# Linear attention in a four-stage fp32 block: values and state as the stationary operand, denominators from running key sums

## The reference

```python
h = _ln(x, g1, beta1)
q = _phi((h @ wq).reshape(b, s, H, DH), proj)     # _phi(x, proj) = elu(x @ proj) + 1
k = _phi((h @ wk).reshape(b, s, H, DH), proj)     # H = 16 heads, DH = 64
v = (h @ wv).reshape(b, s, H, DH)
def step(carry, qkv_t):                           # over the 1024 positions
    kv, ksum = carry
    kv = kv + k_t[..., :, None] * v_t[..., None, :]
    ksum = ksum + k_t
    num = jnp.einsum('bhd,bhde->bhe', q_t, kv)
    den = jnp.einsum('bhd,bhd->bh', q_t, ksum) + 1e-06
    return ((kv, ksum), num / den[..., None])
x = x + outs.reshape(b, s, H * DH) @ wo
```

## Time and profile before

| | |
|---|---|
| median of 3 runs | 3996.98 us (3996.84 to 3997.35) |
| profiled execution, its own time | 3997.76 us |
| its span, first to last instruction | 3995.9 us |
| linear attention, first to last instruction of its loop | 1353 to 2177 us |
| one turn in the steady part | 25.83 us |
| TensorE busy, whole span | 3643.4 us (91%) |
| VectorE, ScalarE, GpSimd busy, whole span | 2522.0, 1601.5, 1392.0 us |

### The profile page before, as it was taken

The page is one execution under the profiler, slowest core; times in us unless marked ns, Lnnn a source line. Parts: engine busy times, 40 slices in busy tenths (PEclk is TensorE's granted clock), DMA queues, the critical chain, the costliest instruction groups (busy, mean ns, idle before and its releaser), DMA issues. The chain is left out here.

```text
span 3995.9 us, 59179 instructions
## 1 busy us (share of the span) xinstructions
PE 3643.4 (91%) x21704; PEld 2593.4 (65%) x21704; DVE 2522.0 (63%) x5386; ACT 1601.5 (40%) x3052; POOL 1392.0 (35%) x1567
## 2 busy tenths in 40 slices
PE   6888878887799999999998998999979989999799
PEld 3666666666455688888886664666645556666465
DVE  4898988899566455555554444777743357777333
ACT  5666666666100122222221213666631146666211
POOL 4778777788100000000000223444411134444111
PEclk8899999999899999999998998999989999999899
DMA  1000000000200100000001112111122011111221
GB/s 39 1 11 12 1 11 11 11 6 6 87 32 32 35 12 12 12 12 12 11 11 55 64 63 64 38 34 37 38 63 64 27 59 33 38 34 34 74 64 37
DMA packets 150197, 129.32 MB, mean 32 GB/s; under 512 B 20804, under 2 KB 147544, under 8 KB 149656
## 3 DMA queue, kind: packets, MB, share of 16 engines
q1 hardware_dynamic: 149912, 125.54, 10.0%
HBM read 87.73 MB, written 37.77 MB: 31 GB/s over the span
## 5 line engine op out<-in xcount | busy, mean ns | idle before, releaser
L830 PEld LDWEIGHTS ssm_pu<-ident,ssm_ub 128*128 128x128 f32 x2048 | 255.8, 150 | 220.3 <-issue 86.0
L830 PE MATMUL ssm_pu<-ident,ssm_ub 128*128 128x128 f32 x2048 | 325.4, 292 | 80.4 <-POOL ssm_ub L322 47.2
L322 POOL TENSOR_SCALAR ssm_ub<-ssm_uT,ssm_bcT 128x512 f32<-128x512 f32 x512 | 356.4, 718 | 96.7 <-ACT ssm_uT L380 63.4
L336 POOL TENSOR_TENSOR ssm_acc<-ssm_acc,ssm_weighted 128x512 f32<-128x512 f32 x256 | 328.4, 1292 | 143.4 <-ACT ssm_weighted L462 143.0
L842 PE MATMUL ssm_pt<-ident,ssm_state 128*128 128x128 f32 x2048 | 288.5, 285 | 82.6 <-DVE ssm_acc L630 58.6
L2256 PE MATMUL win_pa<-win_w_wqkv,win_hT 128*128 128x512 f32 x768 | 357.9, 603 | 1.6 <-ACT win_hT L2043 1.1
L620 DVE TENSOR_TENSOR_SCAN ssm_state<-ssm_da,ssm_carry,ssm_pu 128x512 f32<-128x512 f32 x256 | 312.2, 1260 | 21.2 <-PE ssm_pu L830 16.4
L1838 PE MATMUL glu_up<-glu_hT,glu_w_w 128*128 128x512 f32 x704 | 309.4, 599 | 3.4 <-DVE glu_hT L1761 3.4
L620 DVE TENSOR_TENSOR_SCAN ssm_state<-ssm_da,ssm_pu 128x512 f32<-128x512 f32 x256 | 296.6, 1199 | 25.1 <-PE ssm_pu L830 16.9
L842 PEld LDWEIGHTS ssm_pt<-ident,ssm_state 128*128 128x128 f32 x2048 | 240.4, 147 | 107.9 <-DVE ssm_acc L630 67.8
L2017 POOL TENSOR_TENSOR win_rotated<-win_straight,win_turned 128x512 f32<-128x512 f32 x128 | 163.0, 1274 | 417.0 <-DVE win_turned L2132 417.0
(11 more groups left out here) (241 smaller groups left out, 7295.3 us busy)
## 6 DMA issues: line engine op xcount, KB each, us to landing
win_raw<-in_tables SPq DMA_DIRECT2D x64, 128.0 KB, 2.2
a<-win_y SPq DMA_DIRECT2D x64, 128.0 KB, 1.7
glu_xs<-a SPq DMA_DIRECT2D x32, 256.0 KB, 3.3
glu_x<-a SPq DMA_DIRECT2D x16, 512.0 KB, 5.3
ssm_x<-in_L_attn_x SPq DMA_DIRECT2D x8, 512.0 KB, 3.9
x<-ssm_out SPq DMA_DIRECT2D x16, 256.0 KB, 2.1
moe_x<-x SPq DMA_DIRECT2D x8, 512.0 KB, 3.9
x<-moe_y SPq DMA_DIRECT2D x8, 512.0 KB, 2.9
```

The source lines that it names most:

```text
L322: nc.gpsimd.tensor_scalar(ub[:, i % 2, t, :], uT[:, k % 2, t, :], bcT[:, k % 2, t, n:n + 1], 1.0, ALU.mult, ALU.mult).then_inc(ub_ready.se ...
L336: nc.gpsimd.tensor_tensor(acc[:, k % 2, t, :], acc[:, k % 2, t, :], weighted[:, j, :], ALU.add)\
L830: last = nc.tensor.transpose(pu[c][:, t * P:(t + 1) * P], ub[:, i % 2, t, c * P:(c + 1) * P], ident)
```

## The change

The operands of the numerator products change places. `state[:, r, :]` (now 128x128, 8 blocks of a pair each, off-diagonal halves zero) and `v` (now 64 columns a head) are the stationary operand, queries and scores are the moving one, and the result has features on partitions already. So the turning of `attn` on TensorE and its copy on ScalarE go, and `attn` with them: VectorE writes `attnT` from PSUM with one multiply for each bank of four pairs.

The denominators get a path of their own. VectorE keeps running sums of the keys along the positions (`key_sums`, 8 scans of 128x128 a turn, carried over from the turn before). GpSimd multiplies them with the queries (`weigh_sums`, 2 instructions of 128x512). TensorE adds over the features of each head with a constant 0/1 matrix `of_head` as the stationary operand, 16 columns wide: 8 products, result 16x128. VectorE adds 1e-6 and takes the reciprocal of 16x128. SP sends that to DRAM (8 KB), waits, and loads it back so that each of a pair's 64 partitions has its head's row (two DMAs of 64x8x128, 256 KB each). The multiply waits for both.

`keep` and its loads go: the factor is a constant 0.0 or 1.0 of the instruction. State growth on VectorE is 2 instructions of 64x512 in place of 6 smaller ones. The new tiles lie in `wT`, which is free after the folding of the weights.

The core of the diff:

```diff
+            def widen_reciprocals(turn):
+                sp.wait_ge(rden_ready.sem, rden_ready.at(turn.i))
+                sp.dma_start(rden_sent, rden[:, :]).then_inc(rden_out, 16)
+                sp.wait_ge(rden_out, 16 * (turn.i + 1))
+                sp.wait_ge(attn_ready.sem, attn_ready.at(turn.i - 1))
+                for j in range(2):
+                    sp.dma_start(rden_rows[j * DH:(j + 1) * DH, :, :],
+                                 rden_sent[j:H1:2, :].partition_broadcast(DH)).then_inc(rden_in, 16)
...
+            def weigh_sums(turn):
+                if turn.i:
+                    pool.wait_ge(den_made.sem, den_made.at(turn.i - 1))
+                for g in range(2):
+                    pool.wait_ge(sums_made.sem, sums_made.at(turn.i, g + 1))
+                    pairs = slice(g * GP, (g + 1) * GP)
+                    nc.gpsimd.tensor_tensor(q_k_sums[:, pairs, :], qkT[:, turn.side, 0, pairs, :],
+                                            k_sums[:, turn.side, pairs, :], ALU.mult).then_inc(sums_weighed.sem, 1)
...
+            def key_sums(turn):
...
+                    for r in range(g * GP, (g + 1) * GP):
+                        last = nc.vector.tensor_tensor_scan(
+                            k_sums[:, turn.side, r, :], ones[:, :], qkT[:, turn.side, 1, r, :],
+                            0.0 if begins else k_sums[:, 1 - turn.side, r, P - 1:P], ALU.mult, ALU.add)
...
+                dve.wait_ge(den_made.sem, den_made.at(i))
+                nc.vector.tensor_scalar(den[:, :], pc[2][0:H1, 0:P], 1e-6, None, ALU.add).then_inc(den_kept.sem, 1)
...
+                nc.vector.reciprocal(rden[:, :], den[:, :]).then_inc(rden_ready.sem, 1)
                 if more:
                     features(turn.next())
...
+                for c in range(2):
                     dve.wait_ge(num_ready.sem, num_ready.at(i, c + 1))
+                    dve.wait_ge(rden_in, 32 * (i + 1))
+                    pairs = slice(c * GP, (c + 1) * GP)
+                    nc.vector.tensor_tensor(attnT[:, pairs, :], pc[c][:, :].rearrange("p (r t) -> p r t", t=P),
+                                            rden_rows[:, pairs, :], ALU.mult).then_inc(attn_ready.sem, 1)
...
                 scores_of(turn, 1)
+                scores_of(turn, 0)
+                pe.wait_ge(sums_weighed.sem, sums_weighed.at(i))
+                pe.wait_ge(state_ready.sem, state_ready.at(i - 1))
+                for r in range(PR):
+                    last = nc.tensor.matmul(pc[2][0:H1, 0:P], of_head[:, r, :], q_k_sums[:, r, :],
+                                            start=(r == 0), stop=(r == PR - 1))
+                last.then_inc(den_made.sem, 1)
                 if more:
                     transposes(turn.next())
-                scores_of(turn, 0)
-                if more:
                     queries_keys(turn.next())
...
+                for r in range(PR):
+                    nc.tensor.matmul(pc[r // GP][:, r % GP * P:(r % GP + 1) * P], state[:, r, :], qkT[:, side, 0, r, :],
+                                     start=(r % GP == 0), stop=False, skip_group_check=True)
+                for r in range(PR):
+                    for j in range(2):
+                        last = nc.tensor.matmul(pc[r // GP][j * DH:(j + 1) * DH, r % GP * P:(r % GP + 1) * P],
+                                                v[:, side, 2 * r + j, :], scores[:, 2 * r + j, :],
+                                                start=False, stop=True, skip_group_check=True)
```

More of the change, by code:

```diff
@@ L1287, in body @@
                     front(Turn(turn.pair + 1, turn.side))
+                if more:
+                    weigh_sums(turn.next())
             front(Turn(0, 0))
+            weigh_sums(Turn(0, 0))
             front(Turn(0, 1))
@@ L1410, in body @@
-                dve.wait_ge(keep_in.sems[turn.side], keep_in.at(turn))
-                for c, (lo, hi) in enumerate(BANKS):
-                    dve.wait_ge(delta_ready.sem, delta_ready.at(i, c + 1))
-                    for j in range(2):
-                        half, cols = slice(j * DH, (j + 1) * DH), slice(j * VW, (j + 1) * VW)
-                        bank = pc[c][half, 0:(hi - lo) * 2 * VW].rearrange("p (r e) -> p r e", e=2 * VW)
-                        last = nc.vector.scalar_tensor_tensor(
-                            state[half, lo:hi, cols], state[half, lo:hi, cols], keep[half, turn.side, :],
-                            bank[:, :, cols], ALU.mult, ALU.add)
-                    last.then_inc(state_ready.sem, 1)
+                    dve.wait_ge(rden_in, 32 * (i + 1))
@@ new lines, in body @@
+                    pairs = slice(c * GP, (c + 1) * GP)
+                    nc.vector.tensor_tensor(attnT[:, pairs, :], pc[c][:, :].rearrange("p (r t) -> p r t", t=P),
+                                            rden_rows[:, pairs, :], ALU.mult).then_inc(attn_ready.sem, 1)
+                dve.wait_ge(delta_ready.sem, delta_ready.at(i))
+                for j in range(2):
+                    half = slice(j * DH, (j + 1) * DH)
+                    last = nc.vector.scalar_tensor_tensor(
+                        state[half, :, half], state[half, :, half], kept_on(turn),
+                        pc[2][half, :].rearrange("p (r e) -> p r e", e=DH), ALU.mult, ALU.add)
@@ L1420, in body @@
+                last.then_inc(state_ready.sem, 1)
+                if more:
+                    key_sums(turn.next())
                 if more2:
@@ L1538, in body @@
+                pe.wait_ge(den_kept.sem, den_kept.at(i))
+                for r in range(PR):
+                    for j in range(2):
+                        last = nc.tensor.matmul(pc[2][j * DH:(j + 1) * DH, r * DH:(r + 1) * DH],
+                                                k_rows[:, r, j * DH:(j + 1) * DH],
+                                                v[:, side, 2 * r + j, :], start=True, stop=True)
+                last.then_inc(delta_ready.sem, 1)
                 if more:
                     values(turn.next(), 0)
-                pe.wait_ge(attn_ready.sem, attn_ready.at(i))
```

136 lines of the change are left out of this document (53 added, 83 removed).

## The result

The changed kernel takes 4015.19 us (median of 5 runs, 4013.71 to 4016.4), the kernel before 3996.98 (median of 5). The ratio is 1.0046, with a 95% interval of 1.0035 to 1.0056: slower, by 18 us. The forecast was 4034, 37 us more than before. The sign is right and the time lies in the range, but the loss is half of what was forecast, and it lies just under the forecast's own range of 4016 to 4048.

The account below looks back on a forecast made before the run. TensorE's own list of work, 25.83 us a turn, was taken as the bound. Per turn -2.61 + 3.08 + 0.72 = +1.19, +37 over 31 turns, -1 for the end turns: 4034 us; own range 4016 to 4048, 8 in 10 3997 to 4068.

Parts of the forecast that it names:

- step (a): Numerators on TensorE: 5.40 us before, 1.82 (state part) plus 2.04 (values part) after, a gain of 1.54 a turn.
- step (e): Input's turning moved directly ahead of queries and keys: hT waited for in full, 1.26 us; k_rows chain unchanged.
- step (c): State's growth on TensorE loses its 0.21 us wait for attn: 0.20 us less a turn.
- forecast mechanism: On TensorE, waits for hT and for the reciprocal eat the gain: +1.19 us a turn, 4034 us, chance 0.70.
- (d): Sum over features added to TensorE: 16 records at full price, 1.82 us a turn; from below 0.6.
- (b): The turning of attn removed from TensorE: 0.87 us less a turn.
- R3: Rival: TensorE's clock drops during queries and keys in a third to all of the turns, 4070 to 4145 us; chance 0.09.
- Step (f): VectorE's add and reciprocal (0.28 and 0.74 us) delay the first features and queries and keys' third group: +0.72 a turn.
- free up to 13.7 us: Reciprocals' loads landing up to 13.7 us after queries and keys start cost nothing; expected landing 11.2 us.
- R4: Rival: broadcast loads of the reciprocals land 2.5 to 4 us later than plain ones, 4055 to 4080 us; chance 0.07.

Follow-up runs that it names:

- the wide operand: Changed kernel with the 0/1 matrix of the sum over features padded with zero columns from 16 to 128: 4012.52 us, ratio 1.004.
- the run with the late denominators: Changed kernel with VectorE's two denominator instructions (add, reciprocal) moved behind the features' second group: 4091.89 us, ratio 1.0236.
- the mixed kernel: Changed kernel with each pair's state product next to its two value products, instead of all state products first: 4088.64 us, ratio 1.0229.
- the experiment: Kernel before with only the scale of the k_rows copy made a constant (1.0 or 0.0) instead of a loaded column: 3989.53 us, ratio 0.998.
- the kernel that turns early: Changed kernel with the next input's turning (transposes) moved back between the two halves of the scores: 3964.68 us, ratio 0.9919.

## Why the prediction was half right

**The step that failed** is the pricing of the terms of the sum. A turn was to cost 1.19 us more and costs 0.61 more. The largest miss is step (a), where the 32 records of the values part were priced at 0.064 us each, 2.04 in all; they took 0.056 each, 1.79. Next come the chain of `k_rows` that step (e) called unchanged, 0.17 us shorter, and the growth of step (c), 0.15 us shorter than forecast. The sum is a small difference of large terms (2.61 removed, 3.80 added), so misses of 7 to 13% in three pieces halved it. The waits were forecast where they stood and nearly as long as they were; what they eat was right, and what the new operand order brings was put too low.

**The forecast mechanism holds.** From the turn's start to queries and keys: forecast 6.66, measured 6.51. The handoff (e): forecast 1.26, measured 1.26 (1756.45 to 1757.71), and once more on the kernel before. The sum over features (d): 1.82 taken from the upper bound, 1.85 measured, with the wide operand 1.89; the argument "no partner, full price" was right and the lower bound of 0.6, taken from records that have partners, was not a bound for this case. The turning of `attn` (b) is gone with its 0.87. The loads landed in time. The clock kept its upper level in the steady part, so R3 did not happen in it; the run with the late denominators shows that it does happen in about half of the turns once TensorE waits some 2.5 us in one piece in each.

**The sizes that were off.** The turn was forecast at 27.0 us and is 26.44. The pieces, forecast and measured: up to queries and keys 6.66 and 6.51; queries and keys 8.32 and 8.24; state part 1.82 and 1.88; values part 2.04 and 1.79; growth 1.18 and 1.03; the rest, unchanged, 6.99. Their differences, -0.15, -0.08, +0.06, -0.25 and -0.15, make -0.57 a turn and 18 us of the 19 that were missed. In detail:

- Step (a), the values part, is the largest: 32 records in 1.79 us, 0.056 each, where 0.064 was taken from the window attention. That row holds 16 records and, from start to start, the change to the 128-column operand behind them. At 0.056 a record it leaves 0.12 us for this change, near the 0.17 of the mixed kernel, so dividing by 16 seems to have put the price of the end into the price of a record. Here the growth follows with 64 stationary columns too, and no such change lies at the end of the values part. This explanation fits the rows; no run tests it.
- Step (c), the growth: 0.35 less than before instead of 0.20. The wait explains 0.21. One moving column in 65 less explains 0.02. The other 0.1 would fit a change of shape that is gone, since the values part now has 64 stationary columns as well; no run separates this.
- "It stays at 2.45 us after the turn's start, since its chain is unchanged": it was not unchanged. The copy's scale is a constant now, which the diff shows in the removal of `keep`. While the turning lay in the same wait the copy's length was hidden (all but the 0.07 of the experiment), and the change takes just this cover away. It is 2.31 now, by the start of the products; by that start it was 2.48 before (the 2.45 is that of the weight loads). The prediction named that cover as free time for `hT` and did not see that it also hid the copy.
- Step (f): +0.72 forecast, +0.64 measured. The reciprocal took 0.94, not 0.74. From 8 columns to 128 that is 6.2 ns a column, near the steeper of the two slopes of the earlier trace rows (6.5), not the mean of three points (4.5). (The working's 178 + 120 x 4.5 is 0.72; 196 + 120 x 4.5 gives 0.74.) With the gaps smaller than the 0.04 assumed (VectorE's next instruction starts before the modelled end of the last), the two new instructions held it for 1.17 us (1759.97 to 1761.14) where 1.10 was forecast; the room was 0.47 (to 1760.44, when the exponential could be taken up) where 0.38 was forecast, and the features' first instruction then took 0.35 in place of 0.43. Small misses on both sides cancelled, which was luck. The estimate by the page's repeat count (VectorE: DVE Perf Modes of the Trainium skill, section Walkthrough: the 8-slice pipeline in each mode) was 8.3 ns a column and 1.2 us; this run has it lower.

**What was called hidden was hidden, but by much less.** VectorE's chain behind the numerators was put at 6.6 us against 8.2 of cover. Here it is in one turn, behind the two multiplies:

```profile
1744.33 1.38 DVE L1440 SCALAR_TENSOR_TENSOR lin_state<-lin_state,lin_pc 64x512 f32<-64x512 f32 x2 [0.24 <-PE lin_pc L1564]
1745.74 4.08 DVE L1398 TENSOR_TENSOR_SCAN lin_k_sums<-lin_ones,lin_k_sums,lin_qkT 128x128 f32<-128x128 f32 x8
...
1750.17 1.24 DVE L1369 TENSOR_SCALAR lin_n<-lin_h,lin_rstd 128x256 f32<-128x256 f32 x1
1751.46 0.42 DVE L1407 TENSOR_TENSOR lin_y<-lin_h_keep,lin_pt 128x256 f32<-128x256 f32 x1
```

It ends at 1751.41, and the residual follows at once, 0.26 us after the turn's start, which is just when TensorE's result lets it (before it stood 0.25 us after the turn's start, at 1767.27). The scans took 4.08 us for 8 with a carry, 0.51 each, against 2.4 to 3.6 forecast; the normalisation took 0.9 more for GpSimd's sake. The cover was used up to the last tenth, and the forecast passed by luck there: each further microsecond would have cost 32 us by the prediction's own count. From this follows the wrong bound for the loads. They were "free up to 13.7 us"; by the kernel with late denominators it is about 11.3 there (13.47 less the 2.2 by which the residual came late), and as an estimate 11.9 in the changed kernel, whose queries and keys take 0.64 longer. In the changed kernel they are in at about 10.2 (its reciprocal's end and the 6.7 us measured there), 1.1 us ahead of the numerators' first bank. R4 was a closer rival than its 0.07 said, and the kernel that delayed the loads ran into it.

The last turn: the loads are naked there, as said, and VectorE waits 6.93 us for them, TensorE 4.75. It is shorter than before all the same (20.3 for 21.9 us), because before the clock was lost earlier in it.

## What to carry to other kernels

As this case shows, a transfer between two engines can cost nothing while it lies in another wait, so before you move it, find out what else was hidden in that wait; both prices then come up, as here the handoff (1.26 us) and the copy (0.18). Keep the producer of a cross-engine handoff one independent piece of work ahead of its consumer, and put new instructions of the other engine on the free side of it: one moved call made 4015 us into 3965. When a record's price is read off a short stretch, take the ends out first, and when the cover of a chain is counted, look at what runs beside it on GpSimd.

## What the runs showed of the hardware

- A change between stationary operands of 128 and 64 columns cost 0.17 us (14 of them 2.43 us); for the two changes between 128 and 16 columns at most 0.02 us was left.
- A product of 128 moving columns in fp32 (two records) took 0.23 us with 16 and with 128 stationary columns alike. With 64 and alternating halves it took 0.11; with four neighbours of the same half the values part and the growth together took 3.43 us in place of 2.82.
- The reciprocal took 941 ns for 16x128 (178 to 196 for 4 to 8 columns), the add from PSUM beside it 269.
- A scan of 128 columns took 0.51 us with a start value from memory and 0.46 without (4.08 and 3.70 us for 8), where one of 512 takes 1.2: as an estimate from these two lengths, about 0.2 us of it do not depend on the length.
- A VectorE instruction that took 353 ns alone ended 0.15 us after the end of a GpSimd multiply that had started before it (1241 ns), and took 0.70 us when that was cut in two.
- Two loads of 256 KB, each spreading 4 KB over 64 partitions in pieces of 512 B, landed in 4.2 us (median), the 8 KB before them in 1.3.
- TensorE's clock fell to the 1.2 GHz level for a stretch behind 16 of 31 waits in the kernel with late denominators (2.17 to 3.27 us) and held behind the other 15 (1.02 to 2.75 us), so the wait's length alone does not decide it. It fell behind a wait of 3.74 us in the first turn of the kernel that turns early, and in the last turns behind 1.39 us (before) and 4.75 us (after). Two more traces have the wait of 1.39 us in their last turn and held the clock. With waits of 0.82 and 0.72 us in each turn it stayed at 1.00.
